# Constant matmuls in TensorE's waits, and the last expert's output in two banks, in a four-layer gated cross-attention kernel

## What is computed

```python
logits = x2d @ wg; gates = softmax(logits); idx = argmax(gates)
mask = one_hot(idx); loc = cumsum(mask) - 1; mask = mask * (loc < C)
h = relu(einsum('ecm,emh->ech', dispatched, w1)); eo = einsum('ech,ehm->ecm', h, w2)
out = combine @ eo
```

## Time and profile before

| | us |
|---|---|
| median of 3 runs | 928.03 (927.75 to 930.23) |
| profiled execution, its time | 932.03 |
| profiled execution, its span | 930.2 |
| TensorE busy (matmul) | 839.1, 90% of the span |
| VectorE / ScalarE / GpSimd busy | 454.0 / 327.4 / 207.4 |
| mean granted clock of TensorE | 0.961 |

### The profile page before, as it was taken

One profiled execution on the slowest core, in us unless ns is written; L12 is line 12 of the kernel. 1 busy time (PEld: TensorE's weight loads), 2 busy tenths in 40 slices (PEclk: granted clock), 3 DMA queues, 4 the chain that ended last, 5 costly groups with the idle time before them and its releaser, 6 DMA issues. The chain is left out here.

```text
span 930.2 us, 15103 instructions
## 1 busy us (share of the span) xinstructions
PE 839.1 (90%) x5798; PEld 649.5 (70%) x5806; DVE 454.0 (49%) x1240; ACT 327.4 (35%) x629; POOL 207.4 (22%) x226
## 2 busy tenths in 40 slices
PE   7897999999999997899999999888999995499996
PEld 5675655777888875666666666655777774388885
DVE  2685544420132307577667767755888786000000
ACT  2332222113223223555454545546444441112121
POOL 1115500001425310001000101112765116112212
PEclk8996999999999999999999999999999996599999
DMA  7031910005646347000000000000000012336441
GB/s 229 23 126 35 340 49 23 24 7 199 213 133 216 112 107 273 1 2 1 1 1 1 2 1 1 2 1 2 1 2 1 24 46 86 119 104 201 155 147 20
DMA packets 33873, 70.58 MB, mean 76 GB/s; under 512 B 9218, under 2 KB 23946, under 8 KB 28939
## 3 DMA queue, kind: packets, MB, share of 16 engines
q1 hardware_dynamic: 26937, 59.92, 18.2%
q0 software_dynamic: 6144, 8.31, 4.6%
q10 hardware_dynamic: 722, 1.39, 0.4%
HBM read 54.98 MB, written 14.80 MB: 75 GB/s over the span
## 5 line engine op out<-in xcount | busy, mean ns | idle before, releaser
L593 PE MATMUL banks<-arena 32*120 32x256 f32 (+6 forms) x1808 | 162.2, 377 | 15.5 <-DVE small L1918 12.7
L1233 ACT ACTIVATE arena<-banks 128x512 f32<-128x512 f32 (+4 forms) x185 | 106.9, 597 | 161.8 <-PE banks L1024 33.4
L593 PEld LDWEIGHTS banks<-arena 32*120 32x120 f32 (+5 forms) x1808 | 101.5, 163 | 50.9 <-issue 32.6
L593 PE MATMUL banks<-ffw,arena 128*128 128x256 bf16 (+2 forms) x632 | 117.1, 339 | 0.5 <-issue 0.2
L593 PE MATMUL banks<-arena,ew 128*128 128x256 f32 x512 | 115.7, 385 | 1.4 <-ACT arena L1233 1.4
L593 PE MATMUL banks<-ew,arena 128*128 128x256 f32 x512 | 113.2, 379 | 0.0
L593 PEld LDWEIGHTS banks<-arena,ew 128*128 128x128 f32 x512 | 98.8, 193 | 15.8 <-ACT arena L1233 2.0
L593 PEld LDWEIGHTS banks<-ew,arena 128*128 128x128 f32 x512 | 96.2, 190 | 12.5
L593 PEld LDWEIGHTS banks<-ffw,arena 128*128 128x128 f16 (+1 forms) x640 | 85.2, 136 | 24.9 <-issue 2.6
L1918 DVE TENSOR_REDUCE small<-banks 128x16 f32<-128x1920 f32 x32 | 69.0, 2157 | 20.8 <-PE banks L593 20.7
L1415 ACT ACTIVATE arena<-banks,mcol 120x2048 f32<-120x2048 f32 x32 | 63.1, 1971 | 19.0 <-PE banks L593 19.0
(11 more groups left out here) (240 smaller groups left out, 1243.3 us busy)
## 6 DMA issues: line engine op xcount, KB each, us to landing
ew<-in_w SPq DMA_DIRECT2D x32, 1024.0 KB
xrow<-arena SPq DMA_DIRECT2D x1, 2064.0 KB, 22.0
arena<-xrow SPq DMA_DIRECT2D x8, 258.0 KB, 4.2
zrow<-arena SPq DMA_DIRECT2D x8, 256.0 KB, 2.2
ffw<-in_shared SPq DMA_DIRECT2D x2, 1024.0 KB, 6.2
acc<-x SPq DMA_DIRECT2D x4, 512.0 KB
ffw<-in_tern SPq DMA_DIRECT2D x2, 1024.0 KB, 8.8
out<-x SPq DMA_DIRECT2D x8, 256.0 KB, 2.0
```

Source lines behind the costliest of these rows:

```text
L593: return pe.matmul(o, l, r, start=a, stop=b)
L1233: return nc.scalar.activation(o, i_, ACT.Copy)
```

## The change

A new helper `fill(bank, n)` on TensorE multiplies a 128x128 f32 matrix of ones by itself n times into a bank of PSUM that is free at that point; nobody reads the result. It is called

- at the beginning: 15 times as soon as the ones are set, 4 behind the two weight turns, 12 behind the key row and ahead of the wait for `load["values"]`;
- in `gate_turn(k)`, ahead of the wait for the normalized batch, by the table `FILL`: layer 0: 6 for k = 0, 16 for 6, 18 for 7; layer 3: 8 for 5, 16 for 6, 18 for 7;
- in layer 3's `group_ranks(3)`: 12 ahead of the wait for the picked experts; behind it 40, then a wait for the 16 scatters (`gate_moved`), then 22.

That is 187 in all. Some waits change places so that the constants stand between the wait that frees their bank and the wait for data. Second, the last expert's second half is written to another bank; a new semaphore `half` is raised after its first half, VectorE scales each half on its own and raises `y_sb` after each, and GpSimd scatters each half as it comes.

```diff
--- before.py
+++ after.py
@@ -26,6 +26,7 @@
 CAP = T // E
 ROW = D + E
 XROW = D + 2
+FILL = {0: {0: 6, 6: 16, 7: 18}, 3: {5: 8, 6: 16, 7: 18}}
 GROUPS = [(0, 3), (3, 5), (5, 7), (7, 8)]
 EPS = 1e-5
 NEG = -1e30
@@ -265,7 +266,7 @@
 
         ln_names = "var rstd z zT_ps zT_sb"
         su = sems("setup", "AB_ps AB_sb M_ps M_sb tanh gsum_in gsum_ps gsum_out pick16 parts later "
-                           "wT_ps wT_sb B_ps B_sb col_ps col_sb row_ps row_sb krow tern trow_ps trow_sb")
+                           "wT_ps wT_sb B_ps B_sb col_ps col_sb row_ps row_sb krow consts tern trow_ps trow_sb")
 
         BASE = {0: 0, 3: NB // 2}
         UN = 2 * NB
@@ -277,7 +278,7 @@
         f2 = sems("ffn2", "h_ps h_sb st2 rstd2 hw nT_ps hi lo xb y_ps x")
         sh = sems("shared", "cmp cnt_ps h_ps h_sb y_ps x")
         rt = sems("route", "logit prob_exp prob probs_out rank_in rank_ps hot idx_ps idxf slot_out slot_in sT_ps idx c_ps c_in")
-        ex = sems("experts", "w0 w1 gather0 gather1 gather2 rows0 rows blank xT_ps xT_sb h_ps h_sb y_ps y_sb o0 o1 acc")
+        ex = sems("experts", "w0 w1 gather0 gather1 gather2 rows0 rows blank xT_ps xT_sb h_ps h_sb y_ps y_sb half o0 o1 acc")
 
         block = ctx.enter_context(nc.Block())
         ds = bass.ds
@@ -406,7 +407,7 @@
             g.memset(ones[:, :], 1.0)
             g.memset(onesf[:, :], 1.0)
             g.memset(tri[:, :], 1.0)
-            g.drain()
+            g.drain().then_inc(su["consts"], 1)
 
             g.affine_select(out=tri[:, :], in_=tri[:, :], compare_op=ALU.is_ge, fill=0.0,
                             base=0, pattern=[[1, P]], channel_multiplier=-1)
@@ -581,9 +582,15 @@
             one_gate(3)
             g.wait_ge(s_store, 16 * NB)
             rows_out = out.rearrange("p t n -> (p t) n")
-            for e in range(E):
+            for e in range(E - 1):
                 g.wait_ge(ex["y_sb"], E + e + 1)
                 scatter(e, rows_out, lambda e, j: G3.bitcast(I32)[:, e, j, D:D + 1], E + e, bounds_check=T - 1, oob_is_err=False)
+            g.wait_ge(ex[f"o{(E - 2) % 2}"], 32 * E)
+            for j in range(TB):
+                g.wait_ge(ex["y_sb"], 2 * E + j)
+                g.indirect_dma_start(rows_out, bass.IndirectOffsetOnAxis(ap=G3.bitcast(I32)[:, E - 1, j, D:D + 1], axis=0),
+                                     eout[:, (E - 1) % 2, j, :], None, compute_op=ALU.add, bounds_check=T - 1,
+                                     oob_is_err=False).then_inc(ex[f"o{(E - 1) % 2}"], 16)
             phase_end(g, 1)
 
 
@@ -591,6 +598,11 @@
         def _(pe):
             def mm(o, l, r, a, b):
                 return pe.matmul(o, l, r, start=a, stop=b)
+
+            def fill(bank, n):
+
+                for _ in range(n):
+                    mm(bank[:, 0:P], onesf[:, :], onesf[:, :], True, True)
 
             def turn_weights(bank, n):
 
@@ -623,10 +635,13 @@
                                k == 0, k == KC - 1)
                 m.then_inc(su["row_ps"], 1)
 
+            pe.wait_ge(su["consts"], 1)
+            fill(psum[7], 15)
             pe.wait_ge(load["early"], 16)
             pe.wait_ge(load["fold"], 32)
             for a, n in enumerate(("q0", "k0")):
                 turn_weights(psum[2 + a], n)
+            fill(psum[7], 4)
             pe.wait_ge(su["wT_sb"], 2)
             pe.wait_ge(load["cols"], 16)
             product(psum[4], WT[:, 1], WT[:, 0]).then_inc(su["B_ps"], 1)
@@ -702,9 +717,10 @@
                     m.then_inc(q["y_ps"], 1)
 
                 def gate_turn(k):
-                    pe.wait_ge(gt["z"], b0 + k + 1)
                     if k >= 1:
                         pe.wait_ge(gt["zT_sb"], b0 + k)
+                    fill(psum[6 if L == 0 else 2], FILL[L].get(k, 0))
+                    pe.wait_ge(gt["z"], b0 + k + 1)
                     o = psum[6 if L == 0 else 2].rearrange("p (k n) -> p k n", k=KC)
                     for c in range(KC):
                         for t in range(TB):
@@ -727,10 +743,12 @@
                 def group_ranks(n):
                     t0, t1 = 2 * GROUPS[n][0], 2 * GROUPS[n][1]
                     w = t1 - t0
-                    pe.wait_ge(gt["picked"], n + 1)
                     if n >= 1:
                         pe.wait_ge(gt["rank_sb"], n)
                     pe.wait_ge(one["pT_sb"], b0 + (6 if n == 0 else NB))
+                    if n == 3:
+                        fill(psum[3], 12)
+                    pe.wait_ge(gt["picked"], n + 1)
                     o = psum[4][:, 256:256 + w * E].rearrange("p (t e) -> p t e", t=w)
                     m = mm(o, tri[:, :], sel[:, t0:t1, :], True, False)
                     for t in range(t1 - 1):
@@ -741,8 +759,8 @@
                 def main():
                     pe.wait_ge(su["B_sb"], 1 if L == 0 else 3)
                     if L == 0:
+                        fill(psum[7], 12)
                         pe.wait_ge(load["values"], 32)
-                    if L == 0:
                         keys_values(0)
                     for s in range(NB + 2):
                         lead = L == 3 and s == 0
@@ -764,6 +782,9 @@
                             logits(s - 2)
                     if L == 3:
                         group_ranks(3)
+                        fill(psum[3], 40)
+                        pe.wait_ge(gt["moved"], 16 * NT)
+                        fill(psum[3], 22)
 
                 return keys_values, turn_z, scores, main
 
@@ -918,12 +939,16 @@
                     if i * 2 + u >= 2:
                         pe.wait_ge(q["y_sb"], i * 2 + u - 1)
                     w = ew[:, u, 1, :].rearrange("p (m n) -> p m n", m=MC)
+                    split = i * 2 + u == 2 * E - 1
                     for t in range(TB):
+                        bank = psum[6] if split and t else psum[4 + u]
                         for k in range(MC):
                             if t == 0:
                                 pe.wait_ge(q["h_sb"], i * 2 * MC + u * MC + k + 1)
-                            m = mm(psum[4 + u][:, t * D:(t + 1) * D], heT[:, u, k, t * P:(t + 1) * P], w[:, k, :],
+                            m = mm(bank[:, t * D:(t + 1) * D], heT[:, u, k, t * P:(t + 1) * P], w[:, k, :],
                                    k == 0, k == MC - 1)
+                        if split and t == 0:
+                            m.then_inc(q["half"], 1)
                     m.then_inc(q["y_ps"], 1)
 
                 prepare(BASE[L], 0, 0)
@@ -1859,13 +1884,18 @@
                 v.wait_ge(q["rows"], 16 * (E - 1))
                 for n in range(E):
                     u = n % 2
-                    v.wait_ge(q["y_ps"], E + n + 1)
+                    if n < E - 1:
+                        v.wait_ge(q["y_ps"], E + n + 1)
                     if n >= 2:
                         v.wait_ge(q[f"o{u}"], 16 * E + 32 * (n // 2))
                     for t in range(TB):
-                        m = V.tensor_scalar(eout[:, u, t, :], psum[4 + u][:, t * D:(t + 1) * D], G3[:, n, t, D + 1:XROW],
+                        if n == E - 1:
+                            v.wait_ge(q["y_ps" if t else "half"], 2 * E if t else 1)
+                        bank = psum[6] if n == E - 1 and t else psum[4 + u]
+                        m = V.tensor_scalar(eout[:, u, t, :], bank[:, t * D:(t + 1) * D], G3[:, n, t, D + 1:XROW],
                                             None, ALU.mult)
-                    m.then_inc(q["y_sb"], 1)
+                        if t or n == E - 1:
+                            m.then_inc(q["y_sb"], 1)
 
             first_moe()
 
```

## The result

The changed kernel takes **924.98 us** (median of 11 runs, 923.76 to 926.88) against 928.16 (925.75 to 936.17) for the kernel before on the same chip: ratio 0.9956, 95% interval 0.9937 to 0.9975. That is 3.2 us, 0.34%, just beyond the 0.3% that a measurement tells from no change. The forecast was 922.0 with 918.5 to 926.0: sign and range hold, the size does not. Of the 6.0 us about half came; the time stands near where rival (a) did (924.3).

The account below looks back on a forecast made before the run. Bounds: TensorE, nearly always busy, with low-clock stretches at the start and in one-head layers, plus waits for loads, VectorE and scatters. Gains 0.5 + 1.0 + 1.1 + 1.2 + 2.2 = 6.0 us gave a median of 922.0, range 918.5 to 926.0.

Parts of the forecast that it names:

- rival (a): Last layer: VectorE's 4.4 us wait is in the profiled execution alone; loss of 1.1 there, 924.3 us; chance 0.22.
- Price of a constant matmul: All bursts: two records per constant matmul, 0.23 us at 2.4 GHz and 0.45 at 1.2.
- rival (b): Bursts cost only 0.12 us a matmul, or VectorE slips between GpSimd's adds: about 919 us; chance 0.10.
- (c): Constants do not hold the clock, every burst runs at 0.45 us a matmul: 965 us; chance 0.06 with mixed forms.
- Rival (d): Warm gain and burst overrun cancel everywhere, only the end counts: 925.8 us; chance 0.12.
- Beginning: 0.5 us gained: Kernel start: bursts of 15, 4 and 12 bring the clock back early; first scores at 21.7, not 22.26.
- Burst of 6: 1.0 us gained: Third step: burst keeps the next step warm, saving a 1.3 us difference and costing 0.3 us beyond the idle time.
- First drain: 1.1 us gained: First one-head layer's end: warm TensorE could gain 3.1 us, but VectorE, blocked by GpSimd's adds, limits it to 1.1.
- Last layer: 1.2 us gained: Last drain to first expert: first turn 1.7 us late behind the constants, warm running gives 2.9 back, net 1.2.
- I keep this wait: Last layer: assumes VectorE still sits until 794.74, 4.4 us past the ranks, as in before's profile.
- End: 2.2 us gained: Last expert: halves leave separately, so one VectorE op and one scatter follow the last matmul, saving 2.26 us.
- 4.0 above the median: Whole kernel: profiled execution took 932.03 us against a median of 928.03, so 926.0 if profiled became 922.0.

Follow-up runs that it names:

- the kernel with the end alone: Kernel before plus only the last expert's output in two banks with two scatters, no constant matmul; 928.09 us against 928.61 for before, ratio 0.9984.
- 8 for 22: Changed kernel with 8 constants in place of 22 behind the wait for the scatter of the rows; 922.3 us, ratio to before 0.9925.
- the trimmed one: Changed kernel with gate bursts 5, 12, 15 in layer 0 and 7, 15, 16 in layer 3, 10 for the 12, 8 for the 22; 921.87 us.

## Why the prediction was half right

- **Price of a constant matmul**: right, 0.227 us for 0.23, two records each. That puts rival (b)'s cheaper bursts out, and (c) as well: the clock held at 1.00 through both drains. Rival (d), that only the end counts, is not put out by the times (the constants together give 1.4, with an interval that starts at 0); the traces show gains and losses behind that 1.4, and not bursts without effect.
- **"Beginning: 0.5 us gained"**: failed at "the key row is at 13.75 and ends at 14.75". It started at 13.23, but the clock had just fallen and it took 1.78. 0.2 lost in this execution; in the six others the first scores came near 20.1 to 20.7, and the gain was paid back at 66 to 76. I had taken a clock that is back for one that stays. By the medians the three bursts together give 0.4 (925.43 less 924.98), less than the runs can tell.
- **"Burst of 6: 1.0 us gained"**: the traces say 1.65 (0.2 behind at the scores, 1.43 ahead at the turn of 45.82, before 47.25), but the run without the burst shows the same step warm and the same median. The step that failed was to put the cold stretch of the earlier trace rows down to the 1.08 us idle ahead of it. The medians show no worth of the burst; that it makes the stretch rarer is not ruled out.
- **"First drain: 1.1 us gained"**: right in mechanism, 1.44 by the traces (2.88 - 1.44), with 2.07 us of idle ahead of the count. Of its steps, "these adds begin behind a GpSimd step that does not move" failed: they began at 82.54 for 84.33, 1.79 earlier, which is the lead of 1.44 with which the drain was entered and 0.35 won in it. That 0.35 is what makes 1.44 of the forecast 1.1. And the block was larger than the one copy: three operations, some 1.2 + 0.9 + 1.6 us longer than with the adds cut.
- **"Last layer: 1.2 us gained"**: 0.3 by the traces; rival (a) came true. "I keep this wait" failed: no other profiled execution shows it. The drain gave 1.54 up to the ranks (2.94 - 1.40), not 0.6, since the bursts of 8, 16 and 18 outlast their waits by less than I took. But from the ranks to the second expert's turn pass 22.64 us (809.40 - 786.76), where before's 24.56 (814.26 - 789.70) less the wait of 3.16 are 21.40: 1.2 lost, where rival (a) had 1.1. Against the kernel with the end alone, which has no such wait, the whole stretch from the last layer's step turn gains 0.4 (45.09 for 45.51). The bursts of 40 and 22 are a loss in each pair of traces (0.3 against the kernel without them, whose median, 1.1 over the changed one, says the opposite and settles nothing). 8 for 22 shows what that single count was worth: 2.7 us.
- **"End: 2.2 us gained"**: right, 2.26 by the medians and 2.2 by the traces.
- **Not in the sum**: 1.5 us lost at 194 to 197.4. "Granted clock 1.00 from about 8 us to the end" was wrong there and at 13.1 to 16.5.
- **"4.0 above the median"**: the difference was taken off whole, which was right for the level but not for the gains. Before's profiled execution was slow by the wait (3.2) and, for the other 0.7, I can only point to the clock, whose cold stretches are not the same in each execution. Gains that are read from cold stretches of such a profile are in part a return to its own median; the burst of 6 is the plain case.

The sum as it came, by the traces: -0.2 + 1.65 + 1.44 - 1.5 + 0.3 + 2.2 = 3.9, which with the wait (3.16) is the 7.1 between the two spans; less the 0.7 by which before's profile was slow besides, 3.2. Against the forecast's 6.0 the missing 2.8 are the beginning (0.7), the last layer (0.9) and the stretch at 194 (1.5), with 0.3 more than forecast at the first drain; the 0.65 by which the burst of 6 seemed to give more than forecast goes against the 0.7. That the time still fell within the range is in part luck: the range was drawn to hold rival (a), and the stretch at 194, which no rival had, happened to take no more than was left.

## What to carry to other kernels

A constant matmul that outlasts the wait it stands in is paid for in full, so cut each burst to the wait as the changed kernel's own trace shows it, and most of all where real work is queued behind; but leave no idle time that was not there before, since a burst cut too short gave back at the next wait what it had saved. When one engine is sped up, read what is late next: here VectorE, held by GpSimd's long adds, and cutting these to a quarter changed nothing in the kernel before, while the changed one became 3.6 us faster, some 2.1 of it from that wait. A median that comes out as expected does not show that the mechanism did: follow the lead of one trace over the other from place to place, and see where it grows. Before a wait in a profiled execution is argued with, compare that execution's time with the median of the runs.

## What I had not expected of the hardware

The clock can fall behind work in which TensorE never idled. In the changed kernel's profile the first of these rows stands ahead of the cold stretch at 194:

```profile
190.55 3.98 PE L600 MATMUL banks<-arena 128*128 128x128 f16 x16
194.35 9.43 PE L600 MATMUL banks<-ffw,arena 128*128 128x256 f32 x36
```

Sixteen matmuls of 128 columns take 3.98 us, 0.25 each, and there is a weight load to each (16 loads in 3.69 us). The same 16 stood at 193.42 before, with no fall; of the 11 profiled kernels that hold constants, seven show 0.83 over 190 to 200 and four show 1.00. In the kernel with 8 for 22 and in the trimmed one the 16 start within 0.01 us of each other (190.69 and 190.68), and the 36 records behind them take 9.43 us in one and 7.95 in the other. So the fall stood behind a stretch without idle time, and neither these instructions nor the time at which they run decide whether it comes.

And VectorE's two-source operations and its copy ended, in before's profile, within 0.15 us of the end of whichever add GpSimd was in (89.13 for 89.01, 91.48 for 91.35, 93.71 for 93.69): the wait is as long as what is left of the other engine's instruction, not of its queue.
